# The last layer of a graph network: products held in SBUF between its two stages, on one core

## The reference, cut to what matters

```
def _L3_gnn_ref(x, edge_index, W, b, gamma, beta):
    xw = x @ W.T
    deg  = segment_sum(ones, col)              # with a loop on every node
    dinv = rsqrt(deg)
    msgs = (dinv[row] * dinv[col])[:, None] * xw[row]
    h = segment_sum(msgs, col) + b
    h = (h - mean(h, 0)) * rsqrt(var(h, 0) + 1e-5) * gamma + beta
    h = gelu(h, approximate=False)
    return h + x
x = layernorm(x + _L3_gnn_ref(x, ...), axis=-1)    # so y = 2*x + gelu(...), then layer norm
```

## Time and profile before

| what | value |
| --- | --- |
| median of 3 runs | 4289.04 us |
| lowest and highest | 4285.53 and 4293.08 us |
| the profiled execution's own time | 4288.64 us |
| its span | 4286.9 us |
| mean granted TensorE clock | 0.918 |
| TensorE busy | 3644.7 us, 85% |
| VectorE busy | 2019.5 us, 47% |
| ScalarE busy | 1478.6 us, 34% |
| GpSimd busy | 1471.2 us, 34% |
| moved by DMA | 799.89 MB |

### The profile page before, as it was taken

The page is one execution under the profiler, slowest core; times in us unless marked ns, Lnnn a source line. Parts: engine busy times, 40 slices in busy tenths (PEclk is TensorE's granted clock), DMA queues, the critical chain, the costliest instruction groups (busy, mean ns, idle before and its releaser), DMA issues. The chain is left out here.

```text
span 4286.9 us, 60726 instructions
## 1 busy us (share of the span) xinstructions
PE 3644.7 (85%) x20680; PEld 2223.7 (52%) x20680; DVE 2019.5 (47%) x4003; ACT 1478.6 (34%) x2671; POOL 1471.2 (34%) x1268
## 2 busy tenths in 40 slices
PE   4589994699997999976999999998859999669733
PEld 3134441355554777764677777776635555234432
DVE  7167776433333444366221121112758787157577
ACT  1333332222222444343333333332534444323332
POOL 2455543323111222253333223222536665323111
PEclk6799996799998999998999999999979999889955
DMA  1667767534334656487443433423957765657587
GB/s 65 223 178 199 199 160 243 181 118 144 121 106 151 227 209 213 185 246 236 146 143 128 151 134 135 155 84 120 277 216 258 269 248 205 202 192 237 200 282 279
DMA packets 389308, 799.89 MB, mean 187 GB/s; under 512 B 123014, under 2 KB 123014, under 8 KB 387152
## 3 DMA queue, kind: packets, MB, share of 16 engines
q1 hardware_dynamic: 322000, 577.36, 38.5%
q0 software_dynamic: 67200, 221.25, 17.8%
HBM read 491.80 MB, written 284.56 MB: 181 GB/s over the span
## 5 line engine op out<-in xcount | busy, mean ns | idle before, releaser
L320 PE MATMUL bank<-w_hi,t_r_lo 128*128 128x344 f16 (+1 forms) x2560 | 836.9, 327 | 0.0
L321 PE MATMUL bank<-w_lo,t_r_hi 128*128 128x344 f16 (+1 forms) x2560 | 836.6, 327 | 0.0
L322 PE MATMUL bank<-w_hi,t_r_hi 128*128 128x344 f16 (+1 forms) x2560 | 836.6, 327 | 0.0
L2257 DVE SCALAR_TENSOR_TENSOR t_z<-w_lo,t_z 128x256 f32<-128x256 f32 x640 | 351.2, 616 | 682.5 <-DMA w_lo<-h 652.0
L2226 POOL TENSOR_TENSOR t_r_lo<-t_r,t_r_hi 128x512 f16<-128x512 f32 x320 | 392.8, 1230 | 682.7 <-ACT t_r_hi L2294 679.1
L320 PE MATMUL bank<-l_z_hi,w_lo 128*128 128x512 f16 x960 | 365.4, 381 | 1.5 <-DVE l_z_lo L1765 1.5
L321 PE MATMUL bank<-l_z_lo,w_hi 128*128 128x512 f16 x960 | 365.3, 381 | 0.0
L322 PE MATMUL bank<-l_z_hi,w_hi 128*128 128x512 f16 x960 | 365.1, 380 | 0.0
L1456 POOL DMA_INDIRECT l_z<-sum,slot_i x160 | 160.7, 1004 | 518.4 <-PE bank L1820 437.4
L322 PEld LDWEIGHTS bank<-w_hi,t_r_hi 128*128 128x128 f16 x2560 | 250.7, 98 | 168.2 <-issue 0.3
L2291 ACT ACTIVATE t_r<-bank,vec_scaled 128x512 f32<-128x512 f32 x320 | 219.7, 687 | 326.3 <-PE bank L2322 298.0
(11 more groups left out here) (266 smaller groups left out, 6428.9 us busy)
## 6 DMA issues: line engine op xcount, KB each, us to landing
w_lo<-h SPq DMA_DIRECT2D x160, 512.0 KB, 6.1
h<-b_wide SPq DMA_DIRECT2D x80, 516.0 KB, 2.8
h<-w_hi SPq DMA_DIRECT2D x80, 516.0 KB, 2.6
sum_gat<-a_out SPq DMA_DIRECT2D x80, 514.0 KB
l_x<-x SPq DMA_DIRECT2D x40, 1024.0 KB, 9.0
h<-l_h SPq DMA_DIRECT2D x40, 1024.0 KB, 5.8
b_h<-h SPq DMA_DIRECT2D x40, 1024.0 KB, 6.5
b_x<-x SPq DMA_DIRECT2D x40, 1024.0 KB, 9.1
```

The lines of the kernel that those rows point to most:

```text
L320: pe.matmul(out, s_lo, m_hi, start=(k == 0), stop=False)
L321: pe.matmul(out, s_hi, m_lo, start=False, stop=False)
L322: mm = pe.matmul(out, s_hi, m_hi, start=False, stop=last)
L2257: ins = v.scalar_tensor_tensor(out=z[u][:, s, cols], in0=hrow[:, s, cols], scalar=z[u][:, s, HC + h:HC + h + 1], in1=z[u][:, s, cols], op0 ...
```

## The change

The two stages of the last layer get functions of their own, `gcn_stage` and `output_stage`, and share a list of SBUF places, `Held.rows`: 80 tiles of 128 by 512 float32, one for each group and each m. They lie in the space of weights that are no longer used, in `apart`, in the two bias tiles, in 17 new tiles, and, for the last two groups, in the two `l_x` buffers. ScalarE writes each product straight to its place; the store of `h` and its load are gone, and GELU is applied in place there.

In `gcn_stage` the transposes use four PSUM banks and not two, TensorE, ScalarE and VectorE do the two halves of the turn at m = 1 and m = 3 (before: 2 and 3), `scale(0)` and `scale(1)` run ahead of the loop and `scale(g+2)` stands behind the last statistics of group g, and the load of `x` waits for the first half of `scale` only. In `output_stage` there are four buffers for x; 2x + gelu is written over x, the layer norm is applied by ScalarE (scale and a shift that GpSimd makes from the mean with two further instructions) over it again, and the store goes out from it. The loops over groups are written out and no longer hardware loops. The diff, cut:

```
+class Held:
+    def __init__(self, kn, mem):
...
+        room = room[:(d.groups - 2) * 4] + [self.x[u][:, m, :] for u in range(2) for m in range(4)]
+        self.rows = [room[g * 4:g * 4 + 4] for g in range(d.groups)]
+def gcn_stage(kn, held):
...
+    tp = [kn.bank[n] for n in (0, 1, 6, 7)]
+    mm = [kn.bank[2 + n] for n in range(4)]
+    def sync(sp):
+        for g in range(G):
+            if g >= 2:
+                sp.wait_ge(z_scaled.sem, z_scaled.at((g - 1) * S))
+            sp.dma_start(x[u][:], node_rows(dram["x3"], i, u)).then_inc(x_in[u].sem, 16)
...
+    def vector(dve):
+        scale(0)
+        low_parts(0)
+        scale(1)
+        for g in range(G):
+            for m in range(4):
+                if g + 1 < G and m in (1, 3):
+                    low_parts(g + 1, (m - 1, m))
+                dve.wait_ge(h_done.sem, h_done.at(g * 4 + m + 1))
+                v.bn_stats(kn.bn_stats[:, m, g * 6:(g + 1) * 6], held.rows[g][m][:, 0:real(g)])...
+            if g + 2 < G:
+                scale(g + 2)
...
+    def scalar(act):
+                if g + 1 < G and m in (1, 3):
+                    high_parts(g + 1, (m - 1, m))
+                act.wait_ge(mid.sem, mid.at(g * 4 + m + 1))
+                act.activation(held.rows[g][m], mm[m][:], ACT.Identity, scale=UNSCALE, bias=...)
+    def tensor(pe):
+        def turn(g, chunks=range(4)):
+            pe.wait_ge(z_ready.sem, z_ready.at(g * S + S))
...
+            for m in range(4):
+                if g + 1 < G and m in (1, 3):
+                    turn(g + 1, (m - 1, m))
+                pe.wait_ge(h_done.sem, h_done.at((g - 1) * 4 + m + 1))
+                split_product(pe, mm[m][:], ..., 4).then_inc(mid.sem, 1)
+def output_stage(kn, held):
+    B = 4
+    x = [kn.buffer(mem, f"o_x{b}", [P, S, D], F32) for b in range(B)]
+    def sync(sp):
+        def load(g):
+            if g >= B:
+                sp.wait_ge(stored[b].sem, stored[b].at(16 * (g // B)))
+            sp.dma_start(x[b][:], node_rows(dram["x3"], *divmod(g, 2))).then_inc(x_in[b].sem, 16)
+        for g in range(B - 1):
+            load(g)
+        for g in range(G):
+            if g + B - 1 < G:
+                load(g + B - 1)
+            sp.wait_ge(rows_out.sem, rows_out.at(g * S + S))
+            sp.dma_start(node_rows(dram["out"], *divmod(g, 2)), x[g % B][:]).then_inc(stored[g % B].sem, 16)
+    def gpsimd(pool):
+            norm.pool(pool, i, u)
+            nc.gpsimd.tensor_tensor(shift[:, u, :], norm.moments[:, u, :, 0], norm.power[:, u, :], ALU.mult)
+            nc.gpsimd.tensor_scalar(shift[:, u, :], shift[:, u, :], -1.0, None, ALU.mult)
+    def vector(dve):
+            for s in range(S):
+                v.scalar_tensor_tensor(out=x[b][:, s, :], in0=x[b][:, s, :], scalar=2.0, in1=tp[u][s][:], ...)
+                norm.moments_of(dve, x[b][:, s, :], s, i, u)
+    def scalar(act):
+        apply(0)
+        apply(1)
+        for g in range(G):
+            if g + 2 < G:
+                apply(g + 2)
+            act.wait_ge(shifted.sem, shifted.at(g * 2 + 2))
+            for s in range(S):
+                act.activation(x[b][:, s, :], x[b][:, s, :], ACT.Identity, scale=norm.power[...], bias=shift[...])
-        kn.add(linear_stage(kn, "gcn"))
-        kn.add(norm_coefficients_stage(kn, V_GCN_G, V_GCN_BETA))
-        kn.add(batch_norm_stage(kn, "gcn"))
+        with ExitStack() as mem:
+            held = Held(kn, mem)
+            kn.add(gcn_stage(kn, held))
+            kn.add(norm_coefficients_stage(kn, V_GCN_G, V_GCN_BETA))
+            kn.add(output_stage(kn, held))
```

More of the change, by code:

```diff
@@ L2347, in gat_stage @@
     return {"sync": sync, "gpsimd": gpsimd, "vector": vector, "scalar": scalar, "tensor": tensor}
+class Held:
+    def __init__(self, kn, mem):
+        d = kn.d
+        room = []
+        for w in (kn.w_hi, kn.w_lo):
+            free = w[:, 0:kn.unit_at(W_GCN)].bitcast(F32)
+            room += [free[:, n * D:(n + 1) * D] for n in range(kn.unit_at(W_GCN) // (2 * D))]
+        free = kn.apart[:].rearrange("p t q -> p (t q)").bitcast(F32)
+        room += [free[:, n * D:(n + 1) * D] for n in range(d.tiles * P // (2 * D))]
+        room += [kn.gin_b2[:], kn.fc_b[:]]
+        self.x = [kn.buffer(mem, f"l_x{u}", [P, S, D], F32) for u in range(2)]
+        room += [kn.buffer(mem, f"held{n}", [P, D], F32)[:] for n in range((d.groups - 2) * 4 - len(room))]
+        room = room[:(d.groups - 2) * 4] + [self.x[u][:, m, :] for u in range(2) for m in range(4)]
+        self.rows = [room[g * 4:g * 4 + 4] for g in range(d.groups)]
@@ new lines, in gcn_stage, with two, real, scale @@
+def gcn_stage(kn, held):
+    nc, d, dram, take, pair = kn.nc, kn.d, kn.dram, kn.sig.take, kn.sig.pair
+    G, H = d.groups, d.groups // 2
+    mem = ExitStack()
+    def two(name, shape, dt):
+        return [kn.buffer(mem, f"{name}{u}", shape, dt) for u in range(2)]
+    x = held.x
+    z = two("l_z", [P, S, D], F32)
+    z_hi = two("l_z_hi", [P, 4, D], F16)
+    z_lo = two("l_z_lo", [P, 4, D], F16)
+    tp = [kn.bank[n] for n in (0, 1, 6, 7)]
+    mm = [kn.bank[2 + n] for n in range(4)]
+    x_in = pair("x_in", 16 * H)
+    sum_in = pair("sum_in", 16 * S * H, software=True)
+    z_scaled = take("z_mixed", S * G)
+    z_ready = take("z_ready0", S * G)
+    turned = take("turned0", 4 * G)
+    hi_done = take("hi_done", 4 * G)
+    lo_done = take("lo_done", 4 * G)
+    mid = take("mid", 4 * G)
+    h_done = take("h_done", 4 * G)
+    seen = take("h_seen", 4 * G)
+    def real(g):
+        return d.last_real if g == G - 1 else GROUP
+    def sync(sp):
+        for g in range(G):
+            i, u = divmod(g, 2)
+            if g >= 2:
[3 more added lines that the diff above has]
+        for g in range(G):
+            i, u = divmod(g, 2)
+            if g >= 2:
+                pool.wait_ge(turned.sem, turned.at((g - 1) * 4))
+            for s in range(S):
+                gather_sums(kn, pool, z[u][:, s, :], dram["sum"], g, s, sum_in[u])
+    def vector(dve):
+        v = nc.vector
+        def scale(g):
+            i, u = divmod(g, 2)
+            dve.wait_ge(x_in[u].sem, x_in[u].at(i * 16 + 16))
+            dve.wait_ge(sum_in[u].sem, sum_in[u].at(16 * S * (i + 1)))
+            for s in range(S):
+                dinv = kn.node_dinv[:, g * S + s:g * S + s + 1]
+                v.scalar_tensor_tensor(out=z[u][:, s, :], in0=x[u][:, s, :], scalar=dinv,
+                                       in1=z[u][:, s, :], op0=ALU.mult, op1=ALU.add).then_inc(z_scaled.sem, 1)
+            for s in range(S):
+                dinv = kn.node_dinv[:, g * S + s:g * S + s + 1]
+                dve.wait_ge(z_scaled.sem, z_scaled.at(g * S + s + 1))
+                v.tensor_scalar(z[u][:, s, :], z[u][:, s, :], dinv, None, ALU.mult).then_inc(z_ready.sem, 1)
+        def low_parts(g, chunks=range(4)):
+            u = g % 2
+            for k in chunks:
+                dve.wait_ge(hi_done.sem, hi_done.at(g * 4 + k + 1))
+                v.scalar_tensor_tensor(out=z_lo[u][:, k, :], in0=tp[k][:], scalar=A_SCALE, in1=z_hi[u][:, k, :],
+                                       op0=ALU.mult, op1=ALU.subtract).then_inc(lo_done.sem, 1)
+        scale(0)
[6 more added lines that the diff above has]
+                dve.wait_ge(h_done.sem, h_done.at(g * 4 + m + 1))
+                v.bn_stats(kn.bn_stats[:, m, g * 6:(g + 1) * 6], held.rows[g][m][:, 0:real(g)]).then_inc(seen.sem, 1)
+            if g + 2 < G:
+                scale(g + 2)
+        dve.wait_ge(seen.sem, seen.at(4 * G))
+    def scalar(act):
+        def high_parts(g, chunks=range(4)):
+            u = g % 2
+            for k in chunks:
+                act.wait_ge(turned.sem, turned.at(g * 4 + k + 1))
+                act.activation(z_hi[u][:, k, :], tp[k][:], ACT.Copy, scale=A_SCALE).then_inc(hi_done.sem, 1)
+        high_parts(0)
+        for g in range(G):
+            for m in range(4):
+                if g + 1 < G and m in (1, 3):
+                    high_parts(g + 1, (m - 1, m))
+                own = held.rows[g][m]
+                act.wait_ge(mid.sem, mid.at(g * 4 + m + 1))
+                act.activation(own, mm[m][:], ACT.Identity, scale=UNSCALE,
+                               bias=kn.vec[:, V_GCN_B + m:V_GCN_B + m + 1]).then_inc(h_done.sem, 1)
+    def tensor(pe):
+        def turn(g, chunks=range(4)):
+            u = g % 2
+            pe.wait_ge(z_ready.sem, z_ready.at(g * S + S))
+            for k in chunks:
+                pe.wait_ge(lo_done.sem, lo_done.at((g - 1) * 4 + k + 1))
+                for s in range(S):
+                    ins = pe.transpose(tp[k][:, s * P:(s + 1) * P], z[u][:, s, k * P:(k + 1) * P], kn.ident[:])
+                ins.then_inc(turned.sem, 1)
+        turn(0)
+        for g in range(G):
+            u = g % 2
+            pe.wait_ge(lo_done.sem, lo_done.at(g * 4 + 4))
+            for m in range(4):
+                if g + 1 < G and m in (1, 3):
+                    turn(g + 1, (m - 1, m))
```

(88 more changed lines are left out.)

## The result

The changed kernel takes 4312.39 us (median of 5 runs, 4311.43 to 4314.94) against 4289.53 us for the kernel before: 22.9 us slower, ratio 1.0054, 95% interval 1.0042 to 1.0066. The forecast was 4307 us, slower. Its profiled execution has a span of 4310.6 us, and the mean granted clock is 0.917.

A forecast was written before the change was run, and what follows sets the result against it. TensorE was taken to bound the product stage and SP's queue ring the output stage. The terms 46.6 + 32 - 3.3 - 56.5 = +18.8 on 4288.6 us gave 4307 us, with an 8-in-10 range of 4267 to 4324.

The forecast's parts named there:

- Part 1: Product stage: the earlier turn makes TensorE wait 2.59 us longer for `scale` in each of 18 groups, +46.6 us.
- Part 2: Product stage: TensorE's clock falls once a group behind the longer gap, 1.8 us lost in each of 18 groups, +32 us.
- Rival A: Product stage: the clock holds at 1.00 through the 3.6 us gaps, giving 4275 us, faster; chance 0.20.
- Part 3: Between the stages: without the store of h, VectorE's 3.87 us wait at the meeting mostly goes, -3.3 us.
- Part 4: Output stage: it shortens from 223.2 to 166.7 us, bound by SP's loads and stores at 8.15 us a group, -56.5 us.
- The ring: Output stage: SP issues a new load and store only when the store before has landed, 8.15 us a group.
- Rival B: Output stage: the ring closes faster and VectorE binds, with the clock falling, giving 4283 us; chance 0.09.
- ScalarE's tables: Output stage: 40 changes between GELU and Identity need no further table loads, 0 us.
- rival C: Output stage: ScalarE loads a table at each change, +15 us on top, giving 4323 us; chance 0.05.
- Rival D: Product stage: VectorE is early after all and no transposes wait, giving 4209 us; chance 0.03.

The follow-up runs named there:

- experiment 1: The changed kernel with the two halves of the turn back at m = 2 and m = 3: 4236.88 us, ratio 0.9875.
- experiment 2: The kernel before with one edit, the two halves of the turn at m = 1 and m = 3: 4365.64 us, ratio 1.0175.
- experiment 5: The changed kernel with scale(g+2) ahead of the statistics of product 3, turn still at m = 1 and 3: 4246.51 us, ratio 0.9897.
- experiment 3: The filling: the changed kernel with 16 useless matmuls between product 0 and the turn, groups 1 to 18: 4282.57 us, ratio 0.9981.
- experiment 6: The changed kernel with store(g) before load(g+3) in the output stage, the wait for store(g-1) to land between them: 4283.60 us, ratio 0.9985.
- experiment 7: The changed kernel with store before load in the output stage, the wait for store(g-1) to land kept ahead of store(g): 4283.37 us, ratio 0.9987.

## Why the prediction was right, and where its sizes were off

The forecast was +18.8 us, the result +22.9. The direction came from two losses in the product stage that outweigh the gain in the output stage, and both were shown.

- **Part 1, the turn one product earlier (+46.6).** Right in mechanism, 6 us too large. TensorE's wait begins where product 0 ends and ends with `scale`, as the timeline shows. The term that was off is the start of the transposes: t0 + 5.94 in place of 6.26. Every step on the way is a little shorter (`scale` starts at t0 + 1.53 and not 1.67, its first half takes 2.69 and not 2.78). The prediction had put 0.1 us on the finer waits in `scale` and left it out; how much of the 0.32 is theirs and how much the written-out loop's was not tried. The wait grew from 1.08 to 3.35: 18 x 2.27 = 41. Experiments 1, 2 and 5 take it off or put it on by one small edit each.
- **Part 2, the clock (+32).** Right in mechanism and close in size: 28 from the periods of the filling, 29.8 from its medians. The clock falls for 3.4 us a group, not the 5 assumed, but nearly all of it lies on work, where 1.4 had been put in the gap: two errors that offset each other. The earlier trace rows held the 3.4 already: the shares of its first fall (0.81, three microseconds at 0.50, 0.98) add up to it, where the prediction counted whole microseconds and had 3.8. Rival A (the clock holds, 4275 us) was the one way to the other side, and it is out. The rule of the Trainium skill named there ("TensorE: Matmul & The Clock Gate", section "HAM oscillation — how this bites in real kernels") agrees with this trace: in each of the 18 groups the clock is at 0.50 at most 0.7 us behind the restart.
- **Part 3, no store of h (-3.3).** The wait at the meeting went from 3.87 to 0.15: -3.7.
- **Part 4, the output stage (-56).** The ring was named rightly and sized wrongly, 8.15 us against 9.07. The step that failed is that the second transfer of a pair lands 8.0 us after the first one's issue, whichever goes first; it was taken from a store and a load of the kernel before, where the store went first. That holds for this order in experiment 6 too (0.4 + 7.7 = 8.1). With the load first and the store 0.4 us behind it, the load lands after 6.5 and the store 8.6 after its issue, 9.05 for the pair. Stores 1 to 15 had been put at 15 x 8.15 = 122.3 us and took 135.6 (from 4151.9, where store 0 has landed, to 4287.5), so 13.3 of the 13.6 by which this stage missed (-42.9 against -56.5). (The bounds in the prediction count 17 rings, its sum 15.) Rival B (VectorE binds) is what experiments 6 and 7 make of it.
- **ScalarE's tables: 0.** One load; rival C is out (its sum is 4322, not the 4323 given). The four Identity instructions take the 2.93 us that had been assumed for them. The Trainium skill's sentence that identity is in every set ("ScalarE: Activation LUTs", section "Table sets: the hidden batching unit") holds for GELU here.
- **Rival D** (VectorE early, no wait) fails by the wait list.

By these sizes: 41 + 28 - 3.7 - 42.9, less 1 us for a quicker start of the stage (from the first transpose to the first product 5.07 us against 6.03) is +21.4; the spans differ by 23.7, of which 2.2 lie ahead of the change. Two misses, 10 us too much of loss and 14 us too much of gain, partly cancelled. That the time came out nearer than its terms is luck; that it came out slower is not, since the two terms of loss exceed the gain at their measured sizes too. It is the clock's term that decides it: without its 28 us the same sizes give -7, and experiment 3, where the clock holds, measured -7.3.

Not settled: why a store behind a load lands so late. That the order decides is shown, by which queue or memory it does is not. Nor was it tried why the clock stays low twice as long in two groups of experiment 2.

## What to carry to other kernels

When a step is moved earlier on one engine, look at what it waits for on the others: `scale` kept its place behind the last statistics, so an earlier turn only lengthened TensorE's wait, and 75 us hung on one tuple. A longer wait on TensorE can cost its length and then the half-rate restart, here 2.3 and 1.55 us a group; if the wait can't be shortened, useless matmuls in it can pay. And where a queue holds a load until a store has landed, issue the store first: the same bytes took 6.6 us a group, VectorE's own time, in place of 9.07.

## What the runs showed of the hardware that was not expected

- Useless work made the kernel faster: 288 matmuls in the gaps, 29.8 us less, and half as many the same (4282.57 and 4283.59 us). An idle time of 1.46 us between bursts of 14 us cost no clock in any of 18 groups; one of 3.1 to 3.2 us did, 18 times of 18. Lengths between were not tried in this stage.
- Two transfers of 1 MB issued 0.4 us apart in one queue are not served alike: load first, the pair takes 9.05 us from issue to the second landing, and the store has landed only then; store first, the store lands after 5.2 us and the pair takes 8.1. With the store 4.3 us behind the load the pair takes 8.6.
